# Attention scores of a graph kernel: three bf16 parts of score and maximum summed in PSUM instead of on VectorE

## The reference, cut to what matters

```
h = (x @ W).reshape(N, HEADS, HEAD_DIM)          # 8 heads of 32
alpha_s = einsum('nhc,hc->nh', h, a_src)
alpha_d = einsum('nhc,hc->nh', h, a_dst)
e = alpha_s[src] + alpha_d[dst]                  # one number per edge and head
e = where(e > 0, e, 0.2 * e)
m = segment_max(e, dst)
ex = exp(e - m[dst])
denom = segment_sum(ex, dst)
out = segment_sum(h[src] * ex / denom[dst], dst)
```

## Time and profile before

| | |
|---|---|
| median of three runs | 2691.33 us |
| span of the profiled execution, first to last instruction | 2699.1 us |
| PE busy / VectorE busy / ScalarE busy / GpSimd busy over the span | 73% / 59% / 37% / 52% |
| mean granted TensorE clock | 0.828 of full speed |
| gathers of attention layer 1 | 1304.6 to 1820.4 us |
| gathers of attention layer 2 | 1916.9 to 2430.5 us |

### The profile page before, as it was taken

How to read it: one execution, slowest core, us unless ns; L and a number is a source line. 1 busy time by engine, 2 the same in 40 slices (tenths; PEclk the granted TensorE clock), 3 DMA queues, 4 the chain that set the end, 5 groups by cost and what they waited for, 6 DMA issues and landing times.

```text
span 2699.1 us, 38166 instructions
## 1 busy us (share of the span) xinstructions
PE 1965.3 (73%) x10306; PEld 1549.3 (57%) x10306; DVE 1600.0 (59%) x5094; ACT 994.6 (37%) x2448; POOL 1408.9 (52%) x1415
## 2 busy tenths in 40 slices
PE   7999776676665799996366666675366666665799
PEld 5888644444445799995254454554345454454477
DVE  5200143434337655557378888888478888788744
ACT  4344200000001344443455555552545455452522
POOL 1100277777770234442577777770477777771233
PEclk9999877767775899998678788787778887787789
DMA  5544433333333899996444444440444444440000
GB/s 210 201 187 199 160 105 103 105 104 105 105 104 92 283 353 349 353 342 210 124 143 131 141 134 140 140 134 14 128 134 141 140 137 140 134 143 16 1 24 25
DMA packets 187265, 400.48 MB, mean 148 GB/s; under 512 B 30990, under 2 KB 98130, under 8 KB 180590
## 3 DMA queue, kind: packets, MB, share of 16 engines
q0 software_dynamic: 63520, 179.35, 23.4%
q1 hardware_dynamic: 112302, 187.97, 19.4%
q10 hardware_dynamic: 11232, 30.68, 3.4%
HBM read 323.15 MB, written 75.54 MB: 148 GB/s over the span
## 4 chain that ended last, share of the span: by engine, by line
PE 41%; POOL 23%; DVE 15%; issue 14%; DMA 3%; ACT 3%; DVEq 2%; ACTq 1%; POOLq 0%; SPq 0%
POOL arena L730 13%; POOL arena L1370 10%; PE banks L419 10%; PE banks L1165 9%; PE banks L1488 3%; PE banks L1177 3%; PE banks L1489 3%; DVE arena L1571 2%; DVE arena L1662 2%; PE banks L1459 2%; DMA arena<-ht,srcT 2%; PE banks L1329 1%; ACT arena L1413 1%; DVE arena L1627 1%; PE banks L2081 1%
## 5 line engine op out<-in xcount | busy, mean ns | idle before, releaser
L1370 POOL DMA_INDIRECT arena<-ht,srcT x784 | 793.4, 1012 | 310.8 <-issue 232.5
L730 POOL DMA_INDIRECT arena<-tr,idx1T x392 | 375.8, 959 | 327.0 <-DMA tr<-arena 207.9
L758 PE MATMUL banks<-arena 128*128 x884 | 339.0, 534 | 168.0 <-SPq L737 150.8
L1488 PE MATMUL banks<-arena,XT 128*128 128x264 f32 x884 | 372.3, 512 | 97.0 <-DVE arena L1662 73.2
L758 PEld LDWEIGHTS banks<-arena 128*128 128x128 f32 x884 | 214.3, 262 | 292.4 <-issue 259.6
L1489 PE MATMUL banks<-arena,XT 128*128 128x264 f32 x884 | 344.1, 479 | 0.0
L1662 DVE TENSOR_TENSOR arena<-arena,nrmT 128x528 f32<-128x528 f32 x448 | 312.9, 700 | 19.9 <-ACT nrmT L1435 19.9
L1488 PEld LDWEIGHTS banks<-arena,XT 128*128 128x128 f32 x884 | 211.9, 253 | 164.0 <-DVE arena L1662 83.5
L1413 ACT ACTIVATE arena<-iorow,dlT 128x128 bf16<-128x128 f32 x896 | 267.9, 387 | 65.4 <-issue 65.2
L419 PE MATMUL banks<-parts 128*128 128x512 f32 x1200 | 275.2, 391 | 4.7 <-DVE parts L379 4.7
L781 DVE TENSOR_TENSOR X<-X,banks 128x256 f32 x221 | 91.8, 415 | 312.6 <-PE banks L758 311.7
(11 more groups left out here) (363 smaller groups left out, 3156.7 us busy)
## 6 DMA issues: line engine op xcount, KB each, us to landing
arena<-in_L_ffn_w_dram SPq DMA_DIRECT2D x195, 512.0 KB, 6.0
tr<-arena SPq DMA_DIRECT2D x50, 1024.0 KB, 3.9
XT<-dld ACTq DMA_DIRECT2D x52, 512.0 KB, 4.4
arena<-ht,srcT POOLq DMA_INDIRECT x784
ht<-arena SPq DMA_DIRECT2D x50, 136.0 KB, 1.7
arena<-tr,idx1T POOLq DMA_INDIRECT x392
arena<-ys SPq DMA_DIRECT2D x8, 640.0 KB, 5.9
arena<-in_L_gnn_weight_dram SPq DMA_DIRECT2D x8, 512.0 KB, 9.0
```

Source lines behind the costliest of these rows:

```text
L730: pool.indirect_dma_start(Gr[:, o:o + D], None, TR, bass.IndirectOffsetOnAxis(ap=idx1T[:, q:q + 1], axis=0)).then_inc(d_g[b % NG], 16)
L758: mm = ten.matmul(B[n][:, 0:D], OHr[:, n, h, :], Gr[:, h * D:][:, bass.ds(o, D)], start=(h == 0), stop=(h == 1))
L1370: pool.indirect_dma_start(Gall[:, o:o + ROW], None, HT[L], bass.IndirectOffsetOnAxis(ap=srcT[:, q:q + 1], axis=0)).then_inc(d_g[b % NG], 16)
L1488: ten.matmul(B[n][:, 0:MSG], OH[b][:, 2 * j, :], WG[:, j, 0, :], start=True, stop=False)
```

## The change

In `expand` one register copy serves a whole step, that is both of its groups of edges. In place of one matmul with 48 columns, each group gets three with 16 columns, one for each part of the values; they go to the same 16 columns of PSUM, where they are summed (`start` on the first, `stop` on the last). In `weights_of` two additions (L1640) and two subtractions (L1646) go, as PSUM already holds the sum of the three parts. The table, its columns, the waits and the other engines' programs stay as they are.

```diff
-                for j in range(CC):
-                    t = TB[:, bass.ds(to_.at(c * CH + j // 2), 48)]
-                    mm = ten.matmul(B[4 + j % 2][:, 48 * (j // 2):48 * (j // 2) + 48], OT[b][:, j * P:(j + 1) * P], t,
-                                    start=True, stop=True)
+                for s in range(CH):
+                    o = to_.at(c * CH + s)
+                    for a in range(2):
+                        j = 2 * s + a
+                        for t in range(3):
+                            mm = ten.matmul(B[4 + a][:, 16 * s:16 * s + 16], OT[b][:, j * P:(j + 1) * P],
+                                            TB[:, 16 * t:][:, bass.ds(o, 16)], start=(t == 0), stop=(t == 2))
                 return mm
...
-                pe = PS[:, 4:6, 0:384].rearrange("p b (s c) -> p b s c", c=48)
+                pe = PS[:, 4:6, 0:16 * CH].rearrange("p b (s c) -> p b s c", c=16)
...
                 v = dv.put(vec.tensor_tensor(e4, pe[:, :, :, 0:8], g4, ALU.add))
                 yield
-                for t in (16, 32):
-                    vec.wait_ge(dv.sem, v)
-                    v = dv.put(vec.tensor_tensor(e4, e4, pe[:, :, :, t:t + 8], ALU.add))
-                    yield
                 v = leaky(EE, EE, v)
                 yield
-                for t in (8, 24):
-                    vec.wait_ge(dv.sem, v)
-                    v = dv.put(vec.tensor_tensor(e4, e4, pe[:, :, :, t:t + 8], ALU.subtract))
-                    yield
                 vec.wait_ge(dv.sem, v)
-                vec.tensor_tensor(e4, e4, pe[:, :, :, 40:48], ALU.subtract).then_inc(ee_ok, 1)
+                vec.tensor_tensor(e4, e4, pe[:, :, :, 8:16], ALU.subtract).then_inc(ee_ok, 1)
```

## The result

The kernel with the change took 2710.15 us (median of 4 runs, 2704.62 to 2711.36), the kernel before 2692.16 us (4 runs, 2690.16 to 2696.79): ratio 1.006, with a 95% interval of 1.0046 to 1.0075. That is **18 us slower** (12 to 20); the forecast was 30. The profiled execution took 2711.36 us.

What follows compares the result with a forecast made beforehand. The gather was taken as the bound, 18.7 us a chunk; the loop at 18.17 + 1.75 - 0.65 = 19.27 would exceed it. Both layers 27 us, slow-clock chunks 3: +30 us, 2721 us, range 2697 to 2760.

Steps and rivals of the forecast that it cites:

- The gather bounds the kernel before: In both attention layers, GpSimd's gathers set the period, supplying a chunk every 18.7 us.
- a slack of 0.55 us: The other engines' loop needs 18.17 us a chunk when its data is there, against a period of 18.72.
- VectorE's part: Four instructions fewer between first addition and `adds` shorten a chunk by 0.65 us.
- Register sets at 0.133 us: In TensorE's expansion, each set of register instruction, weight load and matmul costs the sequencer 0.133 us; 24 instead of 16.
- Rival 1: In TensorE's expansion, the added register work is nearly free; chunk 18.0 us, nothing changes, 2689 us; chance 0.09.
- The further pairs: In TensorE's expansion, 24 load and matmul pairs a chunk following another matmul cost the sequencer 0.03 us each.
- 3.41 + 24p: Time in us from first register instruction to next first addition; p is a further pair's sequencer cost, taken as 0.03.
- My lower bound: In TensorE's expansion, a further pair costs at least the array's 0.025 us, giving 1.6 us more a chunk.
- my own sum: The loop's time for a chunk in the attention layers: 18.17 + 1.75 - 0.65 = 19.27 us.
- The late chunks: About ten slow-clock chunks a layer: lateness lies within the longer sequencer time; 0.15 us added on each, 3 us together.
- rival 4: Products behind the expansion fall to the low clock in all chunks, up to 1 us more each; 2755 us; chance 0.07.
- The second chunk of each layer: It waits for data as before and pays only 32 further pairs at 0.025 in its expansion: +0.8 us.

Runs made afterwards that it cites:

- one_register: The kernel before with one register copy for both matmuls of a step instead of one each, 48 columns kept; 2688.21 us, ratio 0.9983.
- double_pairs_2: The changed kernel with each set of three matmuls issued twice, the 24 register instructions a chunk kept; 2729.98 us, ratio 1.0127.
- before_again: The kernel before, unchanged, run once more for a second trace; 2695.43 us, span 2693.7 us.
- tensor_alone: The changed kernel with four VectorE instructions put back (two additions, two subtractions); 2757.02 us, ratio 1.0237.
- light_after_2: The changed kernel with every second gather fetching 64 rows instead of 128; 2719.84 us, ratio 1.0087.
- eight_registers_2: The changed kernel without the two added address instructions of a step, all three matmuls reading the same part; 2687.47 us, ratio 0.9968.

## Why the prediction was right in direction and too high in size

1. **The gather bounds the kernel before: right for a shorter loop; the slack was misread.** Loops of 17.10, 17.26 and 17.72 us all run at 18.61 to 18.63, so this is the supply, and they gain only 4 to 8 us in all. But a slack of 0.55 us was wrong: I took one chunk, 18.17 us; the 31 chunks that are not late have a mean of 18.25, and 21 late ones run at 19.29. With these the kernel before is at 18.67, already 0.06 above the supply: in the mean it had no slack.
2. **VectorE's part: right.** 15.88 to 15.31 us, 0.57 less (predicted 0.65), and the `adds` at 2.08, as predicted.
3. **Register sets at 0.133 us: right.** They start 0.14 apart; with 8, 16 and 24 of them (one_register, before, after) it is 1.42, 2.41 and 3.52 us to the addition in chunks that aren't late, 0.12 and 0.14 for each further one. The address instructions, of which I only assumed it, cost as much as L697, though one takes 46 ns and the other 59. Rival 1 is refuted by this: first to last is 3.2 us where it wanted 2.5, and 8 register instructions instead of 24 take 1.7 us off.
4. **The further pairs: the step that failed.** I put p = 0.03 on each of 24. 3.41 + 24p = 3.52 gives 0.005, and double_pairs_2 0.007 to 0.009. My lower bound, the array's 0.025, was no bound: it holds where the array sets the pace, but here each waited for the sequencer's register work and the pairs went by in its shadow. So the expansion grew by 1.11 us in a chunk that isn't late (2.41 to 3.52), not by 1.75. First to last register instruction is 3.2 us instead of 3.7.
5. **What that would have made of the sum.** With 1.11 my own sum gives 18.17 + 1.11 - 0.65 = 18.63 us, the supply, and no change at all. With the right base and VectorE's 0.57 it is 18.25 + 1.11 - 0.57 = 18.79, and 18.80 is what the 48 undisturbed chunks show. 4 late ones make it 18.90. So it is (18.90 - 18.67) x 52 = 12 us instead of 28. The direction was right by 0.2 us a chunk, less than the 0.64 by which the step was off, so it owes something to luck: with the true cost of the pairs and all else as I had it, I would have forecast no change.
6. **The late chunks: missed, and of the other sign.** I added 3 us for them, took their lateness to vanish within the longer expansion, and gave rival 4 (the low clock spreads) 0.07. They went from 21 to 4. In the changed kernel the products have the whole clock more often (from 1392 to 1830 us a mean of 487 ns for L1491, 506 for the same line, L1488, in before_again, 520 in tensor_alone). A late chunk is 19.29 - 18.25 = 1.04 us longer than the others before, and the four that are left are 20.02 - 18.80 = 1.22 longer all the same: 21 x 1.04 - 4 x 1.22 = 17 us come back of the 52 x 0.55 = 29 that the longer loop costs. Of the lateness before, little is the supply's: ScalarE's waits for gathered data fell by only 4 us in layer 1 (35.2 to 31.1, 6 and 3 waits). Why the products have the full clock more often wasn't tried; double_pairs_2 and light_after_2, with the same VectorE code, have 0 and 1 late chunks.
7. **The second chunk of each layer: right sum, wrong parts.** 1.1 and 0.8 us longer, predicted 0.8. But the expansion there grew by 1.8 in layer 1: from its first matmul to the addition 2.40 us instead of 0.60 (2.28 instead of 0.60 in layer 2). The 0.7 to 0.9 between came back elsewhere in the chunk; VectorE's shorter work, 0.57 a chunk, is most of it if it counts there as in the others, which wasn't measured apart. I had let all register instructions run ahead while products were late. TensorE's sequencer and timeline in that chunk:

```profile
L1462 PEldq FUSED_REGOPS  x6: 46/46/46, 1367.1 to 1371.2; - x6
```

```profile
1371.62 0.61 PE L1492 MATMUL banks<-arena,XT 128*128 128x264 f32 x2
1372.07 2.37 PE L1462 MATMUL banks<-arena,XT 128*128 x48
```

   In the 5 us between 1367.0 and the first expansion matmul, only 9 of the 24 register instructions start (these 6 and 3 of L697, the last at 1371.2), which is 14 to 18 pairs; before, all 16 fitted. Yet a row of the kernel before could have warned me, its register instructions ahead of the second chunk's expansion:

```profile
L697 PEldq FUSED_REGOPS  x16: 53/53/53, 1365.0 to 1369.7; - x16
```

   They took 4.7 us instead of 2.0, from the sixth on mostly 0.44 us apart, which is the pace of the products and not that of register sets: the sequencer was held there already. The Trainium skill (TensorE: Matmul & The Clock Gate, Architectural detail) gives a queue of 64 instructions; here at most 36, loads and matmuls counted apart, stood ahead, and what products still in the queue take of it the trace doesn't tell.
8. **The marks.** Idle time ahead of the first addition 180.3 us (predicted 190); first addition every 18.9 us (19.3); last gather start predicted 5 to 15 us later: from the first gather of a layer to its last it is 515.2 us in layer 1 (515.8 in the first trace, 514.6 in before_again), nothing, and 521.4 in layer 2 (513.6 and 517.4), 4 to 8. That the gather would wait for VectorE was wrong: 1.2 us in 4, as before. It is seen only where the loop is clearly longer, in tensor_alone (23.2 us) and double_pairs_2 (11.0). The stages outside the attention layers should not have moved; they did, by some 4 us, later ahead of the first gather and shorter at the end.

**The better version.** one_register is 4 us faster than the kernel before (0.9983), and so about 21 faster than the changed one (1.006). That eight_registers_2, with all 48 matmuls of the change, is as fast shows that adding in PSUM costs the time through the address instructions, one for each part, and not through the matmuls.

## What to carry to other kernels

Price matmuls with an address from a register by their register instructions; further pairs behind one are almost free as long as the array has time left between the register instructions, so put as many as you can on one address. Before an edit trades one engine's time for another's, take the means of the loop over all chunks, the undisturbed and the late ones apart, and compare them with the supply: a saving below the supply is worth little alone (6 us here), and the same saving is worth its full length, and more (47 us), once a cost elsewhere lifts the loop above it. A margin of 0.06 us between loop and supply can't be read from one chunk.

## What the runs showed of the hardware that was not expected

- A register instruction of TensorE's sequencer takes a set 0.13 to 0.14 us, whether it lasts 46, 53 or 59 ns; 24 further load and matmul pairs in a chunk add some 0.1 us (an estimate, 3.52 measured less 3.41 for the rest), and 48 more 0.35 to 0.42 us.
- A gather of 64 rows holds GpSimd almost as long as one of 128 beside it (medians of 909 and 965 ns).
- In the second chunk TensorE's sequencer ran no more than 14 to 18 pairs ahead of late products; before, all 16 pairs fitted.
- Chunks are late by the clock: 125 of 132 had their products at a mean granted clock of 0.56 to 0.75, all 336 others at 1.00.
- In one comparison TensorE got its instructions in some stretches 0.4 to 1.3 us apart, and the kernel before took 3177.62 us; the cause is open.
